# Attention with a fused FFN on one core: maxima three places ahead, and step-by-step waits for the weights

## The reference, cut to what matters

```python
xn = layernorm(x)                                   # no weights
q, k, v = split(clip(xn @ Wqkv.T, -8, 8), 3)        # Wqkv: 3072 x 1024
q, k = layernorm(q) * q_w + q_b, layernorm(k) * k_w + k_b
# 32 heads of 32 features, per batch
scores = q @ k.T / sqrt(32) + slope[head] * (key - query)
probs = softmax(where(key <= query, scores, -1e30))
attn = (probs @ v) @ Wout.T
ffn = xn @ (alpha * sign(Wf)).T + bias              # alpha: mean |Wf| of each row
return x + attn + ffn
```

## Time and profile before

| | us |
|---|---|
| median of 3 runs | 1325.45 |
| lowest, highest | 1325.14, 1329.71 |
| profiled execution | 1327.45 |
| its span | 1325.4 |

### The profile page before, as it was taken

The page is one execution under the profiler, slowest core; times in us unless marked ns, Lnnn a source line. Parts: engine busy times, 40 slices in busy tenths (PEclk is TensorE's granted clock), DMA queues, the critical chain, the costliest instruction groups (busy, mean ns, idle before and its releaser), DMA issues.

```text
span 1325.4 us, 35664 instructions
## 1 busy us (share of the span) xinstructions
PE 1289.3 (97%) x14628; PEld 640.9 (48%) x14628; DVE 808.0 (61%) x1811; ACT 510.1 (38%) x1018; POOL 574.8 (43%) x360
## 2 busy tenths in 40 slices
PE   5999999998999989999999999999999999999998
PEld 3455444443444434444356655555555555444443
DVE  4656378876877772123688888888888888011111
ACT  6444011111111110000057777777777777600000
POOL 5562000000000000000037777777777777797674
PEclk9999999999999989999999999999999999999999
DMA  6545122222222225922114333444443331344443
GB/s 238 197 159 192 62 71 73 74 77 70 68 77 78 77 80 133 218 72 72 65 50 85 89 87 85 92 99 91 104 100 91 87 90 38 114 140 155 143 144 126
DMA packets 167718, 137.97 MB, mean 104 GB/s; under 512 B 116273, under 2 KB 132785, under 8 KB 167346
## 3 DMA queue, kind: packets, MB, share of 16 engines
q1 hardware_dynamic: 68020, 99.55, 25.2%
q10 hardware_dynamic: 99566, 36.50, 12.3%
HBM read 93.42 MB, written 42.21 MB: 102 GB/s over the span
## 4 chain that ended last, share of the span: by engine, by line
PE 94%; DVE 2%; DMA 1%; issue 1%; POOL 1%; ACT 1%; SPq 0%; DVEq 0%; ACTq 0%; POOLq 0%
PE ps L1085 59%; PE ps L1151 9%; PE ps L1206 9%; PE ps L1229 9%; PE ps L1235 3%; PE ps L1209 2%; PE ps L1074 1%; PE ps L1248 1%; PE ps L1239 1%; DMA arena<-arena 1%; DVE ps L988 1%; DMA arena<-in_x 0%; POOL arena L651 0%; SPq L470 0%; DVE arena L940 0%
## 5 line engine op out<-in xcount | busy, mean ns | idle before, releaser
L1085 PE MATMUL ps<-arena 128*128 128x512 f16 x3584 | 786.9, 381 | 9.3 <-DVE arena L864 9.0
L1085 PEld LDWEIGHTS ps<-arena 128*128 128x128 f16 (+1 forms) x3584 | 348.6, 98 | 434.7 <-issue 15.4
L793 ACT ACTIVATE arena<-ps 128x512 f32<-128x512 f32 (+3 forms) x768 | 333.1, 499 | 122.1 <-PE ps L1209 69.1
L988 DVE CUSTOM_DVE_ANT_0 ps<-ps,arena 128x128 f32<-128x128 f32 (+3 forms) x512 | 238.4, 517 | 37.0 <-PE ps L1151 36.8
L1206 PE MATMUL ps<-arena 128*32 128x512 f16 (+3 forms) x3072 | 256.8, 327 | 3.6 <-DVE arena L940 1.4
L1151 PE MATMUL ps<-arena 127*32 127x512 f16 (+3 forms) x3072 | 237.8, 328 | 0.6 <-DVE arena L988 0.4
L641 POOL TENSOR_TENSOR arena<-arena 128x2048 f32<-128x2048 f32 (+1 forms) x48 | 202.8, 4226 | 37.5 <-ACT arena L793 35.0
L651 POOL TENSOR_TENSOR arena<-arena 128x1536 f32<-128x1536 f32 (+1 forms) x32 | 93.8, 2930 | 262.5 <-PE ps L1229 190.0
L992 DVE TENSOR_REDUCE arena<-ps 128x1 f16<-128x512 f32 x256 | 166.7, 687 | 47.8 <-PE ps L1151 47.7
L564 POOL TENSOR_TENSOR small<-small 128x1 f32<-128x1 f32 x48 | 19.5, 407 | 386.6 <-DVE small L876 384.9
L1229 PE MATMUL ps<-arena 128*32 128x512 f32 (+3 forms) x1536 | 160.6, 486 | 0.5 <-issue 0.3
(11 more groups left out here) (55 smaller groups left out, 848.1 us busy)
## 6 DMA issues: line engine op xcount, KB each, us to landing
arena<-in_x SPq DMA_DIRECT2D x32, 512.0 KB, 5.3
arena<-in_wqkv_t SPq DMA_DIRECT2D x48, 256.0 KB, 6.1
base_scr<-arena SPq DMA_DIRECT2D x16, 512.0 KB, 2.9
v_scr<-arena SPq DMA_DIRECT2D x16, 512.0 KB, 3.0
arena<-r_scr SPq DMA_DIRECT2D x32, 256.0 KB
arena<-base_scr SPq DMA_DIRECT2D x16, 512.0 KB, 4.0
out_dram<-arena SPq DMA_DIRECT2D x16, 512.0 KB, 6.2
arena<-v_scr ACTq DMA_DIRECT2D x14, 512.0 KB, 4.2
```

The costliest lines, as they stand in the source:

```text
L793: nc.scalar.activation(slot(c)[:, j, :], ps[:, TRB[x % RB], 0:w], ACT.Exp, scale=SCALE).then_inc(exp_done, 1)
L988: ins = nc.vector.tensor_tensor_reduce(tile, tile, mnat[:, HALF - width:HALF], scale=-1.0, scalar=3e38, op0=ALU.add, op1=ALU.min, accum_ou ...
L1085: ins = nc.tensor.matmul(dst[c], lhs(k, a), wparts[:, k, b, c * HALF:(c + 1) * HALF], start=(k == 0 and (a, b) == order[0]), stop=(k == KT ...
```

## The change

The natural items run three places (`AHEAD`) ahead: at place i of group n stands item (i + 3) mod 42 of group n+1, and in the last three places items 0, 1 and 2 of group n+2. So item 2, the row-B turn of group n+1, is at place 41 of group n. Items 0 to 2 of group 1 run ahead of attention, on TensorE before its wait for the last V product. The row-B turn of the last group stays at (0, 0) of that group. For Q, K and V the first product waits for two splits ahead of each step.

```diff
+        AHEAD = 3
...
+        def in_group(n, i):
+            return n + 1 + (i + AHEAD) // ITEMS, (i + AHEAD) % ITEMS
...
+            for pos in range(AHEAD):                      # DVE, behind V
+                nat_item(1, pos)
...
             for n in range(GROUPS):                       # DVE
                 for pos in range(ITEMS):
-                    if n < GROUPS - 1:
-                        nat_item(n + 1, pos)
-                    elif pos == 0:
+                    s, item = in_group(n, pos)
+                    if s < GROUPS:
+                        nat_item(s, item)
+                    elif n == GROUPS - 1 and pos == 0:
                         row_out(n, use(GROUPS, 0), row_b, rowb_ld)
...
+            def weights(blk, k):                          # TensorE
+                pe.wait_ge(w_lo, ready(NT * (blk - 1) + 2 * k + 1))
             for blk in (Q, K):
-                pe.wait_ge(w_lo, ready(NT * blk - 1))
+                weights(blk, 0)
                 def step(t, p, j, first=False):
-                    block_product(blk, t, p, tile=p * QT + j)
+                    block_product(blk, t, p, (lambda k: weights(blk, k + 1)) if first else None, p * QT + j)
...
-            pe.wait_ge(w_lo, ready(NT * V - 1))
+            weights(V, 0)
             for t in range(NT):
                 if t < V_FIRST:
-                    block_product(V, t, t % 2)
+                    block_product(V, t, t % 2, (lambda k: weights(V, k + 1)) if t == 0 else None)
...
+            for pos in range(AHEAD):
+                nat_item(1, pos)
...
                         scores(n, c, j)
-                        if n < GROUPS - 1:
-                            for pos in range(due(c, j - 1), due(c, j)):
-                                nat_item(n + 1, pos)
-                        elif (c, j) == (0, 0):
+                        for pos in range(due(c, j - 1), due(c, j)):
+                            s, item = in_group(n, pos)
+                            if s < GROUPS:
+                                nat_item(s, item)
+                        if (n, c, j) == (GROUPS - 1, 0, 0):
                             row_b_turn(n, use(GROUPS, 0))
```

## The result

The changed kernel takes 1340.37 us in the median of four runs (1340.07 to 1340.61), the one before, run beside it, 1327.14 (1325.14 to 1329.71). The ratio is 1.0098, with a 95% interval of 1.0077 to 1.0120: slower by 1.0%. I had forecast 1332.4, slower, with 1339 as the upper end. The sign and the mechanism of the stall hold; the size doesn't, and for one small part the sign doesn't either. The profiled executions took 1327.45 and 1340.44 (spans 1325.4 and 1338.3).

The account below looks back on a forecast made before the run. TensorE was taken to bound nearly everything. Terms of -13.4 - 0.4 + 18.9 + 3.2 - 1.4 = +6.9 us took the profiled 1327.45 to 1334.4; with the runs' median 2.0 lower, 1332.4 us, range 1317 to 1339.

Parts of the forecast that it names:

- the stall: At the row-B turn, groups 3 to 13: line 998 held by POOL's addition, TensorE waiting 1.72 us each, +18.9 us.
- First tile of Q, K and V: At the start of K and V: TensorE's idling for the weights and the clock's fall go, Q gives 0; -13.4 us.
- Groups 0 to 2: First three groups of attention: stalls of +3.2 us, against -1.4 for the excess they had before; +1.8 us.
- Three items before attention: Before attention: three items run in TensorE's 1.4 us wait for line 940; -0.4 us (0 to -1.4).
- The base: Whole kernel before the change: median of the runs 1325.45 us, 2.0 below the profiled execution of 1327.45.
- A (not held): Rival at the row-B turn: line 998 isn't held and K's and V's wait stays gone; 1309.2 us, chance 0.14.
- B (half a stall): Rival in the groups: TensorE makes up some of the stall inside the group; 1321 us, chance 0.10.
- C (the clock falls in the stalls): Rival in the groups: slow matmuls cost 1.6 us in most groups, as behind K's gap; 1355 us, chance 0.03.
- D (K and V keep their gaps): Rival at the start of K and V: something other than the weights is late; 1346 us, chance 0.02.

Follow-up runs that it names:

- the fourth experiment: The changed kernel without line 1003: TensorE turns both halves into PSUM, DVE takes the smaller while copying the row out; 1312.08 us, ratio 0.9888 to the kernel before.

## Why the prediction was right in sign and short in size

**First tile of Q, K and V: right.** -13.4 forecast, -13.3 measured, in the changed kernel, in the one with the weights alone, and in all others with step-by-step waits. The idling and the clock's fall went together, and the counting of 1.6 and 2.8 us of the loss as slow matmuls is borne out: 4.4 of the 13.4.

**The stall: right in its mechanism.** Line 1003 asks 14.52 us behind the mark, by the forecast 14.6; it is held by an addition of 3.5 us just as by the shorter POOL instructions of the earlier trace rows. Taking POOL's addition away and taking the two SBUF operands away each ended it.

**The stall: short in size.** I put 1.72 us on each of groups 3 to 13, and it is 1.84. The wait view gives only 1.56 to 1.63 for each, since it counts from the modelled end of the matmul before; my 1.72 counted from the start of the turn. Counted like that, against the fourth experiment, which has the same order and no hold, the turn of group 3 starts 16.72 us behind the mark (788.32 - 771.60) instead of 14.95 (779.40 - 764.45): 1.77 late. The next mark is 31.89 - 30.07 = 1.82 late. So nearly all of the price lies at the turn, and 0.03 to 0.05 behind it. The forecast had TensorE let go 16.65 us behind the mark (825.66 - 809.01), it was 16.72; and groups without a hold take 30.07 in this order, not 30.05. TensorE's weight loads at line 1164 do wait longer for DVE line 993 in total (12.3 us, 7.5 before), but that hardly reaches its matmuls. Over eleven groups the whole is 1.3 us more than forecast.

**Groups 0 to 2: 3.1 for 1.8.** I had put stalls of 0.2, 1.5 and 1.5 us on them, with POOL's phase taken from the trace of before, where line 998 held and row B late had shifted it. In the changed kernel groups 1 and 2 run like the later ones and group 0 has a shorter hold (1.09 us): they take 30.84, 31.91 and 31.91, so 0.8, 1.9 and 1.9 over 30.05.

**Three items before attention: the wrong sign, +0.9 for -0.4.** That is the step that failed outright, and it failed in two ways.

First, there was nothing to gain. TensorE does use the wait for the last clip of V (0.9 us of it is left, of 1.4), and row B of group 0 does leave sooner: DVE's copy of it starts 2.85 us behind that clip instead of 3.34. I wrote that the wait for its landing therefore doesn't take the gain back. It does. The last of the four DMAs lands 9.98 us behind the clip in the kernel before, and at 9.98 and 9.97 with one and two places ahead. In all of these TensorE starts chunk 4 at 10.0, after a wait for the DMAs of 0.6, 0.7 and 0.5 us. The chain of waits of the kernel before goes through them:

```profile
677.40 3.99 DMA arena<-arena
```

Second, I wrote that DVE takes the items "in the same place of its order as before", and stopped there. With three places DVE is late enough to take the DMAs' place in the chain. It works without a gap for 8 us from 661.73 on. Its items up to chunk 4 were 0 to 13 and are now 0 to 16, two reductions (0.69 us each) and a copy (0.20) more. TensorE is already in group 0 when DVE begins item 0, so from the first item on it waits for banks that DVE has yet to read. The first such wait, in the timeline, and DVE's last reduction in the chain:

```profile
662.53 0.40 PE L1164 MATMUL ps<-arena 127*32 127x512 f16 x4 [0.52 <-DVE arena L993]
```

```profile
667.60 0.32 DVE ps L993
```

Ahead by 0, 1, 2, 3 places the stretch takes 16.03, 16.02, 16.14, 16.95 us, and 17.32 where DVE's row copy is 0.2 us longer as well. So up to two places DVE's extra work fits into time that was spent on row B's DMAs anyway. Of the 0.9 us, 0.27 are a gap on TensorE (at 669.3) for which the profile shows no releaser. That it is DVE is read from the chain and the timeline; no experiment took DVE's work away there.

**The base.** 1325.45 was the median of three runs, 2.0 below the profiled execution; with more runs it came to 1327.14 (4) and 1326.38 (17). The stretch ahead of Q moves by 4.7 us from profile to profile, and +1.9 of the difference of the two profiles is this. Subtracting 2.0 to come from the profile to the median was mostly subtracting noise. With 12.9 - 1.9 = 11.0 us for the change itself, the forecast of 6.9 lacks 4.1: 1.3 of the stall, 1.3 in groups 0 to 2, 1.3 at the start of attention, and 0.1 each in the weights' part and at the end. These 4.1, the 2.0 and the 1.9 are the 8.0 us between 1332.4 and 1340.4. (By the medians the change costs 13.2 us, with 10.2 to 15.9 as the interval, so 11.0 lies within it.) The range ended 1.4 us too low: it allowed 2.0 us a group as the worst of the stall, and named nothing for the base or for a loss at the start of attention.

**Rivals.** A (not held) would need groups of 30.05, and they take 31.89. B (half a stall) is refuted: TensorE makes up nothing of the wait. C (the clock falls in the stalls) is refuted: the granted clock of the span is 0.999, and 1.00 in the 5 us from 788.00 on, behind one of the gaps. D (K and V keep their gaps) is refuted.

**The rule on the shared ports.** The Trainium skill's page "SBUF — State Buffer", section "SBUF: two separate sides", states that the pair of ports shared by GpSimd and VectorE is an exclusive lock for the whole instruction. By that rule, the trace agrees: 2.16 us in the changed kernel and 0.17 in the one without the addition. The Trainium skill's page "GPSIMD Engine Reference", section "8. Key points", speaks of "contention". Read as a shared bandwidth, that would have doubled 0.17 us to about 0.3, and the trace shows 2.16.

## What to carry to other kernels

An instruction of 0.17 us that is moved ahead can land in a place where another engine holds what it needs. Before moving one, lay the three engines over each other at the new place, not only at the old one, and see what ends there: here 15 ends of line 998 with ends of POOL instructions were the warning. Where a small VectorE operation reads two SBUF operands beside long GpSimd work, let it take its operands from PSUM or do it in a copy that is needed anyway. And before a gain is charged for work that moves into a wait, see what ends the next wait of the same chain: here row B's DMAs landed at the same time with none, one and two items ahead of them, and with three DVE became the late one.

## What the runs showed of the hardware

Beside POOL's two-input additions, DVE's instructions with an operand in PSUM (lines 993, 997, 1006) kept their durations (line 997 has a median of 0.68 us beside them and 0.69 without, line 1006 has 0.41 in both cases), and so did the reciprocals with one SBUF operand (0.24). Only the one with two SBUF operands was held, by up to 2.0 us. It goes the other way too: ahead of Q, in the kernel before, a POOL addition of 128x1 elements (line 564) that starts 0.16 us into a DVE subtraction of two SBUF operands (line 893) ends 0.05 us behind it, and takes 1.06 us instead of 0.19. Gaps of 4.5 us in TensorE's work left the granted clock at 0.50 to 0.71 over the next 5 us; 15 gaps of up to 1.6 us, 32 us apart, left it at 0.999 over the span.
